# Linear attention: the turn of the weighted values and the order of VectorE's work in a slot

## The reference

```python
q = x @ Wq + bq;  k = x @ Wk + bk;  v = x @ Wv + bv
k = k @ Wc @ We;  v = v @ Wc @ We
...
qf = elu(q) + 1;  kf = elu(k) + 1
kv = jnp.einsum('bhsf,bhsd->bhsfd', kf, v)
kv_cum = jnp.cumsum(kv, axis=2)
num = jnp.einsum('bhsf,bhsfd->bhsd', qf, kv_cum)
den = jnp.einsum('bhsf,bhsf->bhs', qf, jnp.cumsum(kf, axis=2))[..., None] + EPS
o = (num / den) @ Wo + bo
y = residual + o
return (y - mu) / jnp.sqrt(var + LN_EPS) * gamma + beta
```

## Time and profile before

| | |
|---|---|
| median of 3 runs | 4042.01 us |
| the profiled execution's own time | 4040.42 us |
| its span | 4038.6 us |
| TensorE busy | 3341.6 us, 83% |
| VectorE busy | 2508.9 us, 62% |
| ScalarE busy | 1837.6 us, 46% |
| GpSimd busy | 1083.2 us, 27% |
| TensorE's granted clock, mean | 0.904 of 2.4 GHz |
| the stage's first and last own work | about 3101 to 3321 us of the span |

### The profile page before, as it was taken

The page is one execution under the profiler, slowest core; times in us unless marked ns, Lnnn a source line. Parts: engine busy times, 40 slices in busy tenths (PEclk is TensorE's granted clock), DMA queues, the critical chain, the costliest instruction groups (busy, mean ns, idle before and its releaser), DMA issues. The chain is left out here.

```text
span 4038.6 us, 68059 instructions
## 1 busy us (share of the span) xinstructions
PE 3341.6 (83%) x25583; PEld 2332.7 (58%) x25583; DVE 2508.9 (62%) x6436; ACT 1837.6 (46%) x3033; POOL 1083.2 (27%) x1394
## 2 busy tenths in 40 slices
PE   5999999999999999997878686777565659997996
PEld 3666666666666666665667354556354434444664
DVE  4875775875875875786501698886785751115663
ACT  2565565566565565556533552222232223332453
POOL 2324324225225224326444110000201320004321
PEclk8999999999999999999789787998776769997997
DMA  5434433533533532530155000000000000004430
GB/s 137 116 73 99 113 79 79 126 85 77 129 85 71 134 85 69 129 90 22 63 170 179 29 1 0 1 0 1 5 1 29 1 11 0 0 0 103 98 82 22
DMA packets 177020, 262.18 MB, mean 65 GB/s; under 512 B 19950, under 2 KB 149230, under 8 KB 159694
## 3 DMA queue, kind: packets, MB, share of 16 engines
q1 hardware_dynamic: 152494, 141.06, 12.4%
q10 hardware_dynamic: 19656, 107.37, 12.0%
q0 software_dynamic: 4544, 9.38, 0.7%
HBM read 184.80 MB, written 72.19 MB: 64 GB/s over the span
## 5 line engine op out<-in xcount | busy, mean ns | idle before, releaser
L847 DVE TENSOR_REDUCE enc_mx<-psum 128x2 f32<-128x512 f32 (+1 forms) x1152 | 755.8, 685 | 159.2 <-PE psum L556 156.3
L1013 ACT ACTIVATE enc_e<-psum 128x1024 f32<-128x1024 f32 (+1 forms) x768 | 580.3, 808 | 404.4 <-PE psum L577 311.8
L556 PE MATMUL psum<-enc_ks,enc_qs 80*128 80x128 bf16 (+1 forms) x3072 | 459.9, 254 | 68.9 <-DVE enc_mx L847 55.6
L577 PE MATMUL psum<-enc_qs,enc_ks 83*128 83x256 bf16 (+1 forms) x3072 | 380.1, 249 | 31.8 <-DMA enc_qs<-enc_turned_max 21.9
L556 PEld LDWEIGHTS psum<-enc_ks,enc_qs 80*128 80x128 bf16 x3072 | 223.2, 100 | 188.8 <-DVE enc_mx L847 108.8
L590 PE MATMUL psum<-enc_e,enc_v 128*32 128x256 f32 (+1 forms) x6144 | 330.1, 332 | 0.0
L577 PEld LDWEIGHTS psum<-enc_qs,enc_ks 83*128 83x128 bf16 x3072 | 258.2, 98 | 70.3 <-DMA enc_qs<-enc_turned_max 22.5
L590 PEld LDWEIGHTS psum<-enc_e,enc_v 128*32 128x32 f32 x6144 | 160.4, 109 | 159.5 <-ACT enc_e L1013 52.3
L2749 PE MATMUL psum<-ter_h,weights_b 128*128 128x512 f32 x512 | 224.9, 593 | 2.4 <-DVE ter_h L2800 1.6
L646 PE MATMUL psum<-par_layerr,enc_hidden 128*128 128x128 f32 x1536 | 190.9, 278 | 8.8 <-DVE enc_n_rows L892 8.8
L646 PEld LDWEIGHTS psum<-par_layerr,enc_hidden 128*128 128x128 f32 x1536 | 182.2, 194 | 18.7 <-DVE enc_n_rows L892 12.1
(11 more groups left out here) (529 smaller groups left out, 7240.0 us busy)
## 6 DMA issues: line engine op xcount, KB each, us to landing
enc_qs<-q_pieces ACTq DMA_DIRECT2D x234, 192.0 KB
enc_ks<-k_pieces ACTq DMA_DIRECT2D x234, 192.0 KB
k_pieces<-enc_pieces SPq DMA_DIRECT2D x240, 128.0 KB, 2.0
moe_wb<-moe_w SPq DMA_DIRECT2D x39, 512.0 KB, 4.0
q_pieces<-enc_pieces SPq DMA_DIRECT2D x144, 128.0 KB, 2.0
enc_qs<-q_pieces SPq DMA_DIRECT2D x54, 192.0 KB
enc_ks<-k_pieces SPq DMA_DIRECT2D x54, 192.0 KB
rope_qs<-q_pieces ACTq DMA_DIRECT2D x39, 192.0 KB
```

The costliest lines, as they stand in the source:

```text
L556: last = T_.matmul(p1[f % 2][:, i * kw:(i + 1) * kw], qs[0:KEYED, slot, h, j * P:(j + 1) * P], ks[0:KEYED, slot, h, 0:kw], start=True, sto ...
L577: last = T_.matmul(p2[ch][:, g], ks[0:SCORED, slot, 4 * T + g, ch * P:(ch + 1) * P], qs[0:SCORED, slot, 4 * T + g, 0:n], start=True, stop= ...
L847: V.tensor_reduce(mx[:, u % 2, j * HEADS + h0:j * HEADS + h0 + n], p1[f % 2].rearrange("p (h k) -> p h k", h=n), AX_X, ALU.max)\
L1013: A.activation(e_of(T, ch), p2[ch], ACT.Exp, scale=HD ** -0.5).then_inc(s_e, 1)
```

## The change

The turn of `att` of group k moves from the start of slot k+1 to the end of slot k. On TensorE it stands there between N1's turn and the turn of `both`, both of group k-1. Its move on ScalarE becomes the last of slot k, behind the scaling to `inner`. On VectorE the product and reduction of tile 2 and the last reduction stand ahead of N1's statistics; N2's apply stands between them; the division stands between N1's statistics and N1's apply.

```diff
--- before.py
+++ after.py
@@ -2498,14 +2498,6 @@
             for k in SLOTS_K:
                 if 0 <= k - 1 < GROUPS:
                     g = k - 1
-                    pe.wait_ge(s_att, g + 1)
-                    if g:
-                        pe.wait_ge(N2.s_moved, g)
-                    for t in range(TILES):
-                        last = T_.transpose(bank[6][:, t * P:(t + 1) * P], att[:, t, :], c.ident)
-                    last.then_inc(s_att_t, 1)
-                if 0 <= k - 1 < GROUPS:
-                    g = k - 1
                     pe.wait_ge(s_att_tm, g + 1)
                     if g:
                         pe.wait_ge(s_inner, g)
@@ -2517,6 +2509,8 @@
                 if 0 <= k - 1 < GROUPS:
                     g = k - 1
                     pe.wait_ge(s_y, g + 1)
+                    if g:
+                        pe.wait_ge(N2.s_moved, g)
                     for t in range(TILES):
                         last = T_.transpose(bank[6][:, t * P:(t + 1) * P], y_t[:, t * P:(t + 1) * P], c.ident)
                     last.then_inc(N1.s_rows, 1)
@@ -2535,7 +2529,18 @@
                     if g:
                         pe.wait_ge(N2.s_done, g)
                     N1.turn(pe, g, bank[7])
+                if 0 <= k < GROUPS:
+                    pe.wait_ge(s_att, k + 1)
+                    if k:
+                        pe.wait_ge(N1.s_moved, k)
+                    for t in range(TILES):
+                        last = T_.transpose(bank[6][:, t * P:(t + 1) * P], att[:, t, :], c.ident)
+                    last.then_inc(s_att_t, 1)
+                if 0 <= k - 1 < GROUPS:
+                    g = k - 1
                     pe.wait_ge(N1.s_moved, g + 1)
+                    if k < GROUPS:
+                        pe.wait_ge(s_att_tm, k + 1)
                     pe.wait_ge(s_sum, g + 1)
                     for t in range(TILES):
                         last = T_.transpose(bank[6][:, t * P:(t + 1) * P], both[:, t * P:(t + 1) * P], c.ident)
@@ -2624,22 +2629,22 @@
                 if now:
                     products(k, 1)
                     reduce(k, 1)
-                if 0 <= k - 1 < GROUPS:
-                    N1.statistics(dve, k - 1)
+                    products(k, 2)
+                    reduce(k, 2)
                 if 0 <= k - 2 < GROUPS:
                     if k - 2:
                         dve.wait_ge(N2.s_turned, k - 2)
                     N2.apply(dve, k - 2)
                 if now:
-                    products(k, 2)
-                    reduce(k, 2)
+                    reduce(k, 3)
+                if 0 <= k - 1 < GROUPS:
+                    N1.statistics(dve, k - 1)
+                if now:
+                    divide(k)
                 if 0 <= k - 1 < GROUPS:
                     if k - 1:
                         dve.wait_ge(N1.s_turned, k - 1)
                     N1.apply(dve, k - 1)
-                if now:
-                    reduce(k, 3)
-                    divide(k)
 
         @block.scalar
         def _(act):
@@ -2669,11 +2674,6 @@
                         act.wait_ge(N2.s_normed, k - 2)
                     N2.move(act, k - 2, bank[6])
                 if 0 <= k - 1 < GROUPS:
-                    act.wait_ge(s_att_t, k)
-                    if k - 1:
-                        act.wait_ge(N1.s_rows, k - 1)
-                    A.activation(att_t[:], bank[6], ACT.Copy).then_inc(s_att_tm, 1)
-                if 0 <= k - 1 < GROUPS:
                     act.wait_ge(s_out, k)
                     if k - 1:
                         act.wait_ge(N1.s_rows, k - 1)
@@ -2690,6 +2690,11 @@
                     if k - 1:
                         act.wait_ge(s_sum, k - 1)
                     A.activation(inner[:], bank[7], ACT.Identity, bias=W["beta"], scale=W["gamma"]).then_inc(s_inner, 1)
+                if 0 <= k < GROUPS:
+                    act.wait_ge(s_att_t, k + 1)
+                    if k:
+                        act.wait_ge(N1.s_rows, k)
+                    A.activation(att_t[:], bank[6], ACT.Copy).then_inc(s_att_tm, 1)
     return base
```

## The result

The changed kernel takes 3999.39 us (median of 4 runs, 3989.47 to 4003.72), the kernel before 4041.03 us beside it (4 runs, 4039.39 to 4043.55). The ratio is 0.9892, with a 95% interval of 0.9879 to 0.9906. The mean granted clock of TensorE was 0.91 in the profiled execution, whose span is 3987.7 us.

What follows compares the result with a forecast made beforehand. Slots were bound by hand-overs between engines, neither TensorE nor VectorE full. Savings of 2.7 (k=1), 15.7 (k=2 to 5), 2.6, 1.2 and 2.6 (k=6 to 8) make 24.8 us: 4040.4 to 4015.6, stated as 4017; range 4004 to 4032.

Steps and rivals of the forecast that it cites:

- The order: VectorE's new order in a slot: N2's apply no longer waits behind N1's statistics; called the step that pays.
- T+8.72: T is the end of the transposes of `both`, where a slot starts; N2's turn forecast there instead of T+12.47.
- the turn of `att` is covered: Turn and move of `att`, 1.9 us with hand-overs, fit into TensorE's existing 2.30 us wait for `both`.
- N1's turn to T: Last stretch of a full slot, from N1's turn to the next T: 3.59 us, kept unchanged.
- the case of a slower kernel: Rival: GpSimd holds VectorE's products and reductions, 4.8 us a slot; total 4048 us; chance 0.06.
- The step that failed: TensorE from N2's turn to N1's turn in full slots: 7.40 us, making the slot 19.7 us instead of 23.6.
- The case named as the high clock: Rival: TensorE gets the high clock for longer, so VectorE decides; 36 us saved in all, 4006 us; chance 0.17.
- its 14.1: VectorE's work in a slot would allow N1's turn at T+14.1; TensorE was forecast later, at T+16.12.
- the new wait ahead of the first sums: TensorE at T+3.8 waits 0.6 us for GpSimd's outer product, half done at T+4.47; argued against the high clock.
- Held by the root: Division's last step on VectorE held about 0.2 us beside GpSimd's N1 root; bounds 0 and 1.0 us a slot.
- k=1: Slot k=1: 18.3 us against 21.0, 2.7 saved; slots k=6, 7 and 8 were to save 2.6, 1.2 and 2.6.
- The statement on `tensor_scalar`: VectorE's `tensor_scalar` is not held beside GpSimd's root (1.11 us both times), against the skill; so division's first step not held.

Runs made afterwards that it cites:

- before with filled waits: Kernel before, with identity matmuls (14 and 8) put into TensorE's waits ahead of N2's turn and the turn of `both`: 4065.12 us, ratio 0.9971.
- changed with filled waits: Changed kernel with identity matmuls in TensorE's waits ahead of first sums, N2's turn, turn of `both` and late N1's turns: 4048.78 us, ratio 0.9913.
- the second comparison: Changed kernel run again without edit, against the kernel before: 4006.46 us, ratio 0.9903 (0.9873 to 0.9933).
- the third: Changed kernel run again without edit on the third chip, against the kernel before: 4033.37 us, ratio 0.9886 (0.9871 to 0.9901).

## Why the prediction was wrong

**The order: right.** VectorE's waits for a norm's rows fell from 35.0 to 8.3 us, and none is left ahead of N1's statistics in the full slots. N2's turn starts at T+8.72, as worked out to the hundredth. The Wo product stands right behind the turn of `both`, and the turn of `att` is covered: TensorE waits 1.87 us for `both` behind it. N1's turn to T is 3.56 us (3.59 forecast). All of VectorE's products and reductions took 1.34 to 1.36 us beside GpSimd's work, so the case of a slower kernel, in which they are held, did not come.

**The step that failed** is "From there TensorE has the same work as before less the wait: 1.09 + 6.31 = 7.40, so N1's turn is due at T+16.12". It is the same work, but it took 5.13 us with 0.41 of waiting in it. I kept the durations of a stretch granted 0.63 while removing the 3.4 us wait that stood right ahead of it; in the changed kernel the stretch was granted 1.00. The case named as the high clock, to which I gave 0.17, was the right one: VectorE decides, with 13.85 us to N1's turn against its 14.1. With 17.4 instead of 19.7 us in four slots this makes 9.5 of the 13 us that the stage gained more than forecast.

The full slots (k=2 to 5) of the runs, side by side:

| kernel | wait ahead of N2's turn | N2's turn to N1's turn |
|---|---|---|
| before (both profiles) | 3.4 | 7.1 to 7.8 |
| turn of `att` alone | 3.4 | 6.5 to 8.9 |
| outer product ahead of the root | 2.3 to 3.4 | 6.1 to 7.3 |
| before with filled waits | 0.2 | 7.2, then three times 5.6 |
| changed with filled waits | 0.0 to 1.1 | 5.2 |
| N2's apply on ScalarE | 0.0 | 5.0 |
| division behind N1's apply | 0.1 to 2.0 | 5.0, 5.0, 5.6, 6.2 |
| VectorE's order alone | 0.0 to 0.5 | 5.0 to 5.1 |
| changed (three profiles) | 0.4 to 2.0 | 5.1 |

(In the run with N2's apply ahead of the third product, the stretch has VectorE's third product in it and can't be compared.) The three kernels that wait 2.3 to 3.4 us there never take less than 6.1 us for the stretch; the others mostly take 5.0 to 5.6. The kernel before with filled waits shows it without any move. The wait is not the whole of it: single slots without it ran partly at the low clock, and one wait of 2.0 us had the high clock behind it (5.1 us) and another of 2.0 the low one (6.2). What exactly tips the level stays open.

My reason against that case was the new wait ahead of the first sums. The wait came, longer than I thought (2.81 us instead of 0.6, since the Wo product, at the high clock, is done at T+1.7 and not at T+3.8). But the slow work behind it has slack: N1's rows came at T+9.04 and not at T+8.2, and N1's statistics start only at T+9.75. The changed kernel with filled waits shows this by itself, since its first sums run at the high clock and the slots stay at 17.4. What mattered was which work comes behind the wait that is left. With the outer product ahead of N2's root, 3.4 us of waiting stand in front of the critical sums, and 8.7 us are gone, a part of them by the held VectorE instruction.

**k=0, left out.** I gave it nothing. By the earlier trace rows the division's last step took 2.40 us there. In the changed kernel ScalarE's copy of the last sums, and so GpSimd's product, comes behind the move of `att`, and the step takes 0.69: 1.5 us saved.

**Held by the root: wrong, without effect.** I had 0.2 us for the division's step beside GpSimd's root. It took 0.69 us, the undisturbed duration, though it started while the root was still running (3189.30, with the root from 3188.64 to 3189.65). What is left of the excess is k=1 (0.8 more than forecast), k=7 (0.3) and k=8 (0.9). k=6 was right.

**The statement on `tensor_scalar`: too wide.** I wrote that the trace does not agree with the Trainium skill ("SBUF — State Buffer", section "Who interferes with whom") that a `tensor_scalar` can be blocked. My statement holds for the root (1.11 us beside it). Beside the wide outer product a `tensor_scalar` took 0.92 us for 0.17 and 1.64 for 1.11, so there the runs agree with the Trainium skill. On two SBUF inputs they agree with it beside GpSimd's wide products alone: beside the root the division's step was not held (0.69 us). The changed order puts no `tensor_scalar` in that place, so it cost nothing here.

**The total.** 42 us in the first comparison are 37.8 of the stage and 4 that the stage does not explain. The stage alone would make a ratio of 1 - 37.8/4041 = 0.9906, or 4004 us from the 4042 that the forecast started from: the edge of the range. That the measured 3999 lies outside it is scatter on top of the failed step; the second comparison, 4006, lies inside. Of the three intervals for the changed kernel the second holds 0.9906, the first has it at its edge, and the third ends at 0.9901, just below.

## What to carry to other kernels

Where a change removes a wait of TensorE, price what comes behind the wait at both clocks, and look where the wait that is left will stand: if the slow stretch falls on work with slack, the gain can be well above the wait removed. Ask next which engine bounds the loop at the high clock; here it was VectorE (busy 64.3 of 69.6 us), with TensorE so close behind that 1.0 us less on VectorE shortened a slot by 0.2 on average. When stages outside the change scatter by more than the change's parts, measure the stage itself.

## What the runs showed of the hardware

- A `tensor_scalar` on VectorE is held beside GpSimd's 128x576 product (0.92 us for 0.17, 1.64 for 1.11), and not beside its 128x4 root of 1.0 us (1.11). The 0.92 us one ended at 3209.51, 0.02 us behind the first half of that product (3208.31 to 3209.49). A division step with two SBUF inputs took 2.40 us instead of 0.69 beside the 128x1152 product in k=0, and 0.69 beside the root.
- Two levels of the clock within one slot: the same four sums take 2.29 us behind a wait of 2.81 us, at the lower level (1.2 GHz, granted 0.50), and 1.14 us at the higher one (2.4 GHz, granted 1.00) 4.7 us later. In the run with the `att` move alone the first sums take 1.24 us behind a wait of 2.80 us.
- Filler on TensorE is not free: 14 matmuls of 64 columns took 3.24 us in one wait (granted 1.00) and 6.23 in another (granted 0.50), where they delayed what they were to speed up.
